# Graph attention on one core: the row scores get two bank pairs, the transposed scores keep one, and both mask products stand ahead of the result's turn

## The reference

```python
normed = layer_norm(x, gamma1, beta1)
qkv = normed.reshape(b_, n_, H, HD).transpose(0, 2, 1, 3)      # 8 heads of 16
scores = jnp.einsum('bhqd,bhkd->bhqk', qkv, qkv) * scale
masked = jnp.where(adj_matrix[:, None, :, :] > 0, scores, -jnp.inf)
attn = jax.nn.softmax(masked, axis=-1)
out = jnp.einsum('bhqk,bhkd->bhqd', attn, qkv)
x = x + out.transpose(0, 2, 1, 3).reshape(b_, n_, d_)
```

## Time and profile before

| | |
|---|---|
| Median of 3 runs | 2775.05 us (2774.55 to 2778.54) |
| Profiled execution | 2770.89 us, its span 2769.0 us |
| TensorE busy over the span | 2675.4 us, 97% |
| VectorE, ScalarE, GpSimd busy | 1938.7, 1461.0, 1506.1 us |
| Attention phase, by the rows below | first row maximum at 22.7 us, last one at 520.8 us |
| TensorE's granted clock in the steady part of the phase | 1.00 |

### The profile page before, as it was taken

The page is one execution under the profiler, slowest core; times in us unless marked ns, Lnnn a source line. Parts: engine busy times, 40 slices in busy tenths (PEclk is TensorE's granted clock), DMA queues, the critical chain, the costliest instruction groups (busy, mean ns, idle before and its releaser), DMA issues. The chain is left out here.

```text
span 2769.0 us, 85746 instructions
## 1 busy us (share of the span) xinstructions
PE 2675.4 (97%) x28783; PEld 2143.5 (77%) x28784; DVE 1938.7 (70%) x6630; ACT 1461.0 (53%) x2930; POOL 1506.1 (54%) x2542
## 2 busy tenths in 40 slices
PE   8999999899979999999999899998998999999999
PEld 4666666599967888888878677777778999999888
DVE  6777777477778888888888577777864455544453
ACT  3555445455546666666666454444554444444444
POOL 5555555233335555555555447776752666666664
PEclk9999999999999999999999999999999999999999
DMA  1111111000000000000000011111422222222264
GB/s 53 35 34 34 34 31 47 2 0 0 0 2 0 0 0 0 0 0 0 0 0 0 21 41 58 58 54 54 129 72 67 78 77 76 77 78 81 70 202 143
DMA packets 158117, 118.26 MB, mean 43 GB/s; under 512 B 20150, under 2 KB 145593, under 8 KB 158010
## 3 DMA queue, kind: packets, MB, share of 16 engines
q1 hardware_dynamic: 140602, 81.02, 10.5%
q0 software_dynamic: 17408, 35.95, 3.8%
HBM read 68.36 MB, written 48.56 MB: 42 GB/s over the span
## 5 line engine op out<-in xcount | busy, mean ns | idle before, releaser
L2027 POOL DMA_INDIRECT token_y<-e_y,e_rows x288 | 295.2, 1025 | 78.8 <-issue 72.1
L2070 ACT ACTIVATE e_hidden<-e_ps,e_b1g 128x512 f32<-128x512 f32 x288 | 194.6, 688 | 258.3 <-PE e_ps L90 257.7
L1303 POOL DMA_INDIRECT sorted_z<-r_z,r_rows x256 | 263.8, 1031 | 67.2 <-issue 62.8
L842 POOL TENSOR_TENSOR s_sw<-s_expo,s_rsum 128x512 f32<-128x512 f32 x128 | 133.6, 1044 | 297.3 <-DVE s_rsum L1100 297.3
L2122 PE MATMUL e_ps<-expert_w,e_hidden 128*128 x2304 | 280.3, 275 | 0.0
L2122 PEld LDWEIGHTS e_ps<-expert_w,e_hidden 128*128 128x128 f32 x2304 | 273.9, 192 | 6.3
L514 DVE TENSOR_REDUCE a_V<-a_ps_s 128x8 f32<-128x1024 f32 x128 | 156.9, 1226 | 129.6 <-PE a_ps_s L394 129.6
L2199 DVE TENSOR_TENSOR e_biased<-e_ps,expert_b 128x512 f32<-128x512 f32 x72 | 49.8, 691 | 213.9 <-PE e_ps L2122 213.9
L394 PE MATMUL a_ps_s<-a_nT 16*128 16x128 f32 x2048 | 184.9, 298 | 0.1
L402 PE MATMUL a_ps_st<-a_topT,a_nT 17*128 17x128 f32 x2048 | 183.6, 297 | 0.1
L394 PEld LDWEIGHTS a_ps_s<-a_nT 16*128 16x128 f32 x2048 | 135.6, 187 | 45.5 <-issue 45.2
(11 more groups left out here) (400 smaller groups left out, 8094.8 us busy)
## 6 DMA issues: line engine op xcount, KB each, us to landing
e_z<-sorted_z SPq DMA_DIRECT2D x72, 260.0 KB
c_y<-token_y SPq DMA_DIRECT2D x22, 512.0 KB, 4.1
X<-in_x_dram SPq DMA_DIRECT2D x32, 256.0 KB, 2.8
a_adj<-in_adj_dram SPq DMA_DIRECT2D x32, 256.0 KB, 2.8
g_adj<-in_adj_dram SPq DMA_DIRECT2D x32, 256.0 KB, 2.9
out_dram<-X SPq DMA_DIRECT2D x32, 256.0 KB, 2.5
c_y_s<-token_y SPq DMA_DIRECT2D x10, 512.0 KB, 4.9
token_y<-e_y,e_rows POOLq DMA_INDIRECT x288
```

Of the source, the lines that this page charges most:

```text
L842: nc.gpsimd.tensor_tensor(sw[p][:, :, :], expo[p][:, :, :], rsum[p][:, 1, :].unsqueeze(2).to_broadcast([T, HEADS, C]), ALU.mult).then_inc( ...
L1303: nc.gpsimd.indirect_dma_start(sh.sorted_z, bass.IndirectOffsetOnAxis(ap=rows[own][:, e * GB + piece:e * GB + piece + 1], axis=0), zr[own] ...
L2027: nc.gpsimd.indirect_dma_start(sh.token_y, bass.IndirectOffsetOnAxis(ap=rows[p][:, b:b + 1], axis=0), y[p][:, b, :], None).then_inc(y_scat ...
L2070: nc.scalar.activation(hidden[p][:, c, :], ps_1[c % 2][:, :], ACT.Gelu, bias=b1g[p][:, c:c + 1]).then_inc(s["hidden_done"], 1)
```

## The change

Three edits. The bank pairs are dealt out the other way: `ps_s` becomes two pairs (by `b % 2`), `ps_st` one. The order on TensorE becomes: turn n, row mask, transposed mask, turn of the result. And the waits follow: the row mask no longer waits for the row maximum, its wait for `nT_done` moves behind the turn of the result, and the transposed mask waits for the exponential of the graph before (`k - 2` in place of `k - 3`). No instruction of the four compute engines is added or removed. Because the row mask now stands first, L365 in the changed code is what was L376, L373 what was L366, and every line below is lower by one to three.

```diff
-        ps_s, ps_st = ps("a_ps_s", [T, 2, 4, T]), [ps(f"a_ps_st{i}", [T, 2, 4, T]) for i in range(2)]
+        ps_s, ps_st = [ps(f"a_ps_s{i}", [T, 2, 4, T]) for i in range(2)], ps("a_ps_st", [T, 2, 4, T])
...
-                        nc.scalar.activation(probT[b % 2][:, :, :, :], ps_st[b % 2][:, :, :, :], ACT.Exp,
+                        nc.scalar.activation(probT[b % 2][:, :, :, :], ps_st[:, :, :, :], ACT.Exp,
...
-                    if live(kk, 2, n_graphs):
-                        own, i = (p, b - 2) if b >= 2 else (q, b + 2)
-                        if since(kk, 4):
-                            pe.wait_ge(s["prob_done"], k - 3)
-                        for c in range(2):
-                            nc.tensor.matmul(ps_st[b % 2][:, c, :, :], edge_bias[own][:, i, :],
-                                             sh.ident_bf[:, :].unsqueeze(1).to_broadcast([T, 4, T]),
-                                             start=True, stop=False)
                     if live(kk, 0, n_graphs):
                         if b == 0:
                             pe.wait_ge(s["bias_done"], t - 1)
-                        pe.wait_ge(s["nT_done"], k + 1)
-                        if since(kk, 1):
-                            pe.wait_ge(s["top_done"], k)
                         for c in range(2):
-                            nc.tensor.matmul(ps_s[:, c, :, :], sh.ident_bf[:, :],
+                            nc.tensor.matmul(ps_s[b % 2][:, c, :, :], sh.ident_bf[:, :],
                                              edge_bias[p][:, b:b + 1, :].to_broadcast([T, 4, T]),
+                                             start=True, stop=False)
+                    if live(kk, 2, n_graphs):
+                        own, i = (p, b - 2) if b >= 2 else (q, b + 2)
+                        if since(kk, 3):
+                            pe.wait_ge(s["prob_done"], k - 2)
+                        for c in range(2):
+                            nc.tensor.matmul(ps_st[:, c, :, :], edge_bias[own][:, i, :],
+                                             sh.ident_bf[:, :].unsqueeze(1).to_broadcast([T, 4, T]),
                                              start=True, stop=False)
...
+                    if live(kk, 0, n_graphs):
+                        pe.wait_ge(s["nT_done"], k + 1)
                     if live(kk, 2, n_graphs):
                         pe.wait_ge(s["topT_done"], k - 1)
```

More of the change, by code:

```diff
@@ L339, in keep_warm @@
                 for i in range(count):
-                    nc.tensor.matmul(ps_st[0][:, i % 2, :, :], sh.ident_bf[:, :],
+                    nc.tensor.matmul(ps_st[:, i % 2, :, :], sh.ident_bf[:, :],
                                      sh.ident_bf[:, :].unsqueeze(1).to_broadcast([T, 4, T]), start=True, stop=True)
@@ L393, in step @@
                                     side = nT[p][32 * tile:32 * tile + HD, b, c, :]
-                                    last = nc.tensor.matmul(ps_s[:, j, 2 * half + c, :], side, side, start=False,
+                                    last = nc.tensor.matmul(ps_s[b % 2][:, j, 2 * half + c, :], side, side, start=False,
                                                             stop=(half == 1 and c == 1))
@@ L401, in step @@
                                     rows = slice(32 * tile, 32 * tile + HD + 1)
-                                    last = nc.tensor.matmul(ps_st[b % 2][:, j, 2 * (1 - half) + c, :], nT[own][rows, i, c, :],
+                                    last = nc.tensor.matmul(ps_st[:, j, 2 * (1 - half) + c, :], nT[own][rows, i, c, :],
                                                             topT[(b + 2) % 4][rows, c, :], start=False,
@@ L514, in step @@
                         nc.vector.reduce_max(V[p][:, b, :, TOP].rearrange("p (c i j) -> p j i c", c=2, j=2),
-                                             ps_s[:, :, :, :].rearrange("p j (i c) n -> p j i c n", c=2), AX.X).then_inc(s["top_done"], 1)
+                                             ps_s[b % 2][:, :, :, :].rearrange("p j (i c) n -> p j i c n", c=2), AX.X).then_inc(s["top_done"], 1)
             run_steps(dve, step, groups, LAG, PEEL)
```

## The result

The changed kernel takes 2750.94 us (median of 4 runs, 2749.09 to 2753.76) against 2775.66 us of the kernel before on the same chip (4 runs, 2774.55 to 2778.54): 24.7 us less, a ratio of 0.9904 with a 95% interval of 0.9879 to 0.9928. A second set of runs gave 2751.63 us and 0.9917 (0.9903 to 0.9931), about 23 us. The profiled execution took 2749.09 us with a span of 2747.3, against 2770.89 and 2769.0.

The account below looks back on a forecast made before the run. A ring of TensorE and VectorE through the row maximum was taken as the bound. Gains of 22.2 us (steady steps) plus 0.8 (edges), less half a microsecond, gave 22.5 off 2775.05: 2752.5 us, range 2746 to 2767.

Parts of the forecast that it names:

- ring through the row maximum: Old kernel's bound: mask product, score products, row maximum, next mask product; 3.898 us a step, TensorE standing 0.20 us.
- third edit could win nothing: Moving the nT_done wait to the first score product: nothing to win, since it leaves L376, where TensorE stood anyway.
- possible loss on L393: First score product gets a second, long-given semaphore: zero expected, 6 us at the outer end, half a microsecond taken off.
- rival with a hand-over of 0.14 from ScalarE: Exponential to transposed mask: ordinary steps take 3.74, gain 17 us, time 2758; longer exponential ring (10 to 20 us) had 0.22.
- The new ring: Through ScalarE, transposed mask waiting for the previous graph's exponential: closes in 3.60 + 0.08 = 3.68 us.
- TensorE's order: TensorE's own sequence from transposed mask to transposed mask: 3.26 + 0.43 = 3.69 us, a floor.
- The rule on rotating banks: Skill page against the change: transposed scores lose bank rotation, so the exponential would be exposed; timeline agreed only on a bound.
- Return and late steps: Once in eight steps the loop's return gains 0.07, the next step 0.14, others 0.21; mean gain 0.184 us.
- The edges: Start and end of the attention phase: +0.8 at the start, some 0.2 each twice, -0.18 each twice; together +0.8 us.
- The other phases: Phases after attention: as long as before, with the clock unchanged at 1.00.
- The covers: Slack costed at nothing: 0.18 for the result's turn, 0.13 for L430 behind VectorE's division, the thinnest.
- rivals: Longer exponential ring (gain 10 to 20 us) 0.22; gain taken elsewhere (0 to 10) 0.12; slower 0.06.

Follow-up runs that it names:

- order-only kernel: Kernel before with the new mask order (row mask, then transposed mask) but the old bank pairs and their waits; two runs, 2819.27 and 2849.80 us.
- moved wait alone: Kernel before with only the row mask's wait for nT_done moved behind the result's turn, banks and order kept; 2765.81 us, ratio 0.997.
- kernel without row mask: Changed kernel without the row mask product, row maxima taken over unmasked scores; 2748.24 us, ratio 0.9901.
- extra activation: Changed kernel with one more ScalarE activation, a 128x128 SBUF copy, right before the exponential; 2773.90 us, ratio 0.9996.
- halved exponential: Changed kernel with the exponential as two activations of 512, each matmul of the transposed mask waiting for its own half; 2754.13 us, ratio 0.9913.
- spare waits out: Changed kernel, in the hardware loop without five TensorE waits that an earlier wait already implies; 2751.49 us, ratio 0.9912.
- filled gap: Changed kernel with 18 instead of 4 idle products at the start of graph 0's step, where TensorE stood idle; 2743.95 us, ratio 0.9889.
- second-wait kernel: Changed kernel with a second, long-given wait for nT_done in front of prob_done at the transposed mask; 2758.79 us, ratio 0.9941.

## Why the prediction was right

- **What bounds before.** The ring through the row maximum: right as a ring, and the order-only kernel shows it at work. Of the step's 0.20 us of waiting, though, 0.09 came from the second wait on L376, which I took for the hand-over of VectorE. The moved wait alone brings ordinary steps from 3.90 to 3.82. The prediction did not need to know, since the change removes the whole wait; but its sentence that the third edit could win nothing holds only beside the new banks. Alone, this edit, which I had costed only as a possible loss on L393, brings 8.6 us; they are no part to be added to the 24.7, since the new banks remove the same wait. The rival with a hand-over of 0.14 from ScalarE had no ground in VectorE's 0.14, which was a matter of where the wait stood.
- **The new ring.** Predicted to close in 3.68 with a hand-over of 0.08. Measured is 3.67 to 3.68 where nothing of TensorE covers it (the kernel without row mask), but with a hand-over to the matmul of 0.05 to 0.06; the 0.08 of ordinary steps of the changed kernel is only when TensorE gets there. So the size of the ring was right and its last term 0.02 to 0.03 too large. TensorE's order: predicted 3.69, measured 3.69 to 3.70. That the two lie side by side is shown from both sides.
- **The rule on rotating banks** (the Trainium skill, Perfetto Trace Analysis, Optimizing Tensor Performance). By the trace the lost rotation cost no time in ordinary steps, but it is what makes the 0.2 us of the extra activation cost the whole gain. With the old order the same single pair costs 0.23 us a step more than before. So the rule held as a warning, and the work between the exponential and its mask decided.
- **Return and late steps.** 3.84 and 3.74 beside the predicted 3.83 and 3.76. But late steps come twice in eight, so the mean gain is (3.898 - 3.725) = 0.173 and not 0.184: 20.9 us over 121 steps instead of 22.2. I had put the exponential's lateness at 306.61 down to the loop's return, but it stands in the trace of the kernel before in every fourth step, 0.08 each, and the cause can be read there too. ScalarE's copy and exponential have two waits each, the deciding one written first. Of the copy's, in the changed kernel:

```profile
L318 ACTq EVENT_SEMAPHORE  x96: 17/17/17, 44.6 to 502.2; - x96
L318 ACTq ALU_OP  x28: 35/35/35, 57.8 to 460.3; - x28
```

In 96 steps the copy itself waits for the turn and the other wait stands ahead of it; in the 28 first steps of a group in the loop, register arithmetic carries the deciding wait and the copy starts 0.07 later. The exponential does the same. No run removes the arithmetic, so this rests on the rows alone. The halved exponential removes what both late steps cost.
- **The edges.** This term was mis-sized: predicted +0.8, measured -1.9. The first steps did lose the wait of 0.80, but the clock stayed at its lower level longer, from 21 to 41 us instead of from 22 to 36 (a step at that level takes 5.3 to 6.7 us): the stretch began 2.10 us later. Behind it 0.24 us came back. The sum, 20.9 - 2.10 + 0.24 = 19.0, is 534.7 - 515.7 taken apart. Whether the change makes the lower level last longer is not shown: there is one trace of the kernel before, and the two of the changed kernel differ by 1.6 us there (its second gives 17.5 for the phase).
- **The other phases.** Predicted to stay as long as before. The other 2.7 us of the profiled pair lie in the MLP phase, whose code is the same: it takes 253.0 us in one trace and 250.3 in the other, and all kernels profiled here show 249.9 to 250.4 or 252.1 to 253.0 for it, without regard to the change. The clock goes with it: in the 14 traces TensorE stood at its lower level for 14.6 to 18.2 us of the short ones and for 20.9 to 27.1 us of the long ones. So of the 21.8 us between the profiled executions 19.0 fall into the attention phase. That 2752.5 came so close to 2750.94 is therefore luck in part: the steady stretch gave 20.9 instead of 22.2, the edges -1.9 instead of 0.8, and the MLP phase, which the prediction held to be unchanged, 2.7 more.
- **The covers.** L381 never waited in its matmuls in the stretch. L508 ends 0.26 us before L429 in the step with the four L488, predicted 0.27. The second wait on L393 is free (spare waits out). None of the rivals came about in the changed kernel; the exponential's ring with the hand-over of 0.14 is what a second wait makes of it, 7 us.

## What to carry to other kernels

When a wait at the head of a mask product is the bound, ask not only which buffer to double but what stands between the reader's end and the next write: here two pairs for one score tile and an exchange of two products with equal cost gave 23 to 25 us, while either alone lost 0.23 and 0.37 us a step. On an instruction that waits for two semaphores, see in the trace which wait it carries itself and which became an instruction ahead of it: the one that comes last should be waited for alone, or the other moved to where TensorE is busy. What is saved at one wait is small (0.09 us), but on a ring it is saved in every step. And read a start-up phase apart from the steady one: a filled gap of 2.6 us was worth 7.7.

## What the runs showed of the hardware that I had not expected

- A hand-over to TensorE takes 0.05 us to the weight load from ScalarE, and as much from VectorE, when the instruction has one wait. Where the deciding wait stands on an instruction ahead of the load it is 0.11 to 0.12 to the load and 0.14 to 0.15 to the matmul (the kernel before in all steps, the second-wait kernel in three of four, the moved-wait and order-only kernels in the fourth). L381 of the changed kernel shows the other way round that two waits by themselves do not cost it: the deciding one is written first, and the load starts 0.05 after the copy's end in 99 steps of 127, and 0.12 to 0.21 after it in the other 28, each of them the first of a group, where register arithmetic carries the deciding wait.
- Waits that are spare, with their register arithmetic, cost nothing while matmuls stream, and 0.06 to 0.1 us at a hardware loop's return (3.84 against 3.78 or 3.74).
- ScalarE's copy `a_topT` and the exponential behind it come 0.07 to 0.08 us late every fourth step, where register arithmetic carries the wait that decides.
- TensorE's granted clock went from 1.00 to 0.50 after an idle gap of 2.6 us that ended at 20.3 us, and came back at about 41 us in the changed kernel; in the kernel before the gap was 3.0 us and the clock was back at about 36. With the gap filled it did not fall before the phase's end. How late it comes back varies: 46 us in the second profile of the changed kernel, where the MLP starts 1.6 us later with the same steady step (3.728 and 3.727), and 60 us in the second-wait kernel.
